# Two PSUM banks for q's projection, squares beside the norms, and a gate from the hyperbolic tangent

## What is computed

```
xn = layernorm(x)                              # x: 2 x 512 rows of 512
q, k, v = xn Wq^T, xn Wk^T, xn Wv^T            # 32 query heads, 8 key/value heads of 128
q, k = rmsnorm(q) * wq, rmsnorm(k) * wk        # t * (mean(t^2) + 1e-6)^-1/2 * w
attn = softmax(q k^T / sqrt(128) + causal ALiBi bias)
s    = (attn v) Wo^T
g    = silu(2 * sum_h (xn A_h^T) B_h^T * 8 softmax(xn Wr^T + br)_h)
y    = x + s * g
```

## Time and profile before

| | |
|---|---|
| time, median of 3 (lowest, highest) | 797.04 us (796.98, 799.42) |
| the profiled execution: its time, its span | 793.71 us, 791.6 us |
| mean granted clock of TensorE | 0.983 |
| busy: PE, PEld | 727.6 us (92%), 612.6 us (77%) |
| busy: DVE, ACT, POOL | 583.8 us (74%), 559.6 us (71%), 399.9 us (51%) |
| DMA | 148 MB, 187 GB/s, queue 64.7% of 16 engines |

### The profile page before, as it was taken

The page is one execution under the profiler, slowest core; times in us unless marked ns, Lnnn a source line. Parts: engine busy times, 40 slices in busy tenths (PEclk is TensorE's granted clock), DMA queues, the critical chain, the costliest instruction groups (busy, mean ns, idle before and its releaser), DMA issues.

```text
span 791.6 us, 14475 instructions
## 1 busy us (share of the span) xinstructions
PE 727.6 (92%) x3729; PEld 612.6 (77%) x3729; DVE 583.8 (74%) x1378; ACT 559.6 (71%) x1370; POOL 399.9 (51%) x423
## 2 busy tenths in 40 slices
PE   8888989999899999999899989999899998999697
PEld 7777867778788778887778778887787787787575
DVE  7855778677886778687877769778786778777555
ACT  4664767686676877777777876777686866768863
POOL 5313373555444762544644664445635554447347
PEclk9999999999999999999999999999999999999989
DMA  7014848678495767859485765858477784956642
GB/s 285 1 28 115 270 107 237 191 214 239 109 275 156 223 185 194 240 145 294 130 236 169 231 201 151 270 153 258 130 224 205 208 251 109 268 159 188 187 148 94
DMA packets 214772, 148.01 MB, mean 187 GB/s; under 512 B 48992, under 2 KB 205536, under 8 KB 214624
## 3 DMA queue, kind: packets, MB, share of 16 engines
q1 hardware_dynamic: 214752, 147.77, 64.7%
HBM read 85.84 MB, written 61.87 MB: 187 GB/s over the span
## 4 chain that ended last, share of the span: by engine, by line
PE 33%; issue 26%; POOL 24%; DVE 10%; ACT 4%; DMA 2%; POOLq 1%; SPq 1%; DVEq 0%; ACTq 0%
POOL pt_lo L529 10%; POOL inv_rms L519 8%; PE qkv_ps L1151 7%; PE qkv_ps L1152 6%; PE qkv_ps L1153 6%; POOL wo_lo L511 3%; DVE qk_norm L963 3%; DVE sums L947 2%; PE score_ps L1151 2%; PE score_ps L1153 2%; POOL sums_eps L517 2%; PE score_ps L1152 2%; PE out_ps L1151 2%; PE out_ps L1152 2%; PE out_ps L1153 2%
## 5 line engine op out<-in xcount | busy, mean ns | idle before, releaser
L529 POOL TENSOR_TENSOR pt_lo<-x_sb,pt_hi 128x512 fp32r<-128x512 f32 x153 | 195.3, 1303 | 240.8 <-ACT pt_hi L691 240.8
L1151 PE MATMUL qkv_ps<-w_hi,xt_hi 128*128 128x512 f32 (+1 forms) x512 | 182.0, 355 | 40.4 <-DVE qk_norm L963 38.4
L1152 PE MATMUL qkv_ps<-w_lo,xt_hi 128*128 128x512 f32 (+1 forms) x512 | 176.9, 345 | 0.0
L1153 PE MATMUL qkv_ps<-w_hi,xt_lo 128*128 128x512 f32 (+1 forms) x512 | 175.8, 343 | 0.0
L639 ACT ACTIVATE probs<-probs,neg_max 128x128 f32<-128x128 f32 (+3 forms) x256 | 141.7, 556 | 37.4 <-DVE neg_max L899 35.0
L1151 PEld LDWEIGHTS qkv_ps<-w_hi,xt_hi 128*128 128x128 f32 x512 | 99.2, 194 | 70.2 <-DVE qk_norm L963 34.6
L899 DVE CUSTOM_DVE_ANT_0 probs<-score_ps,cst,slope 128x128 f32<-128x128 f32 (+3 forms) x196 | 102.0, 545 | 54.1 <-PE score_ps L1153 46.1
L647 ACT ACTIVATE probs<-probs,recip 128x128 f32<-128x128 f32 (+3 forms) x252 | 122.2, 549 | 6.1 <-DVE recip L906 6.0
L918 DVE STREAM_TRANSPOSE squared<-probs 128x256 f32<-128x256 f32 (+3 forms) x124 | 99.7, 823 | 18.9 <-ACT probs L647 17.0
L1152 PEld LDWEIGHTS qkv_ps<-w_lo,xt_hi 128*128 128x128 f32 x512 | 99.6, 195 | 11.9
L1153 PEld LDWEIGHTS qkv_ps<-w_hi,xt_lo 128*128 128x128 f32 x512 | 99.2, 194 | 12.0
(11 more groups left out here) (166 smaller groups left out, 1444.7 us busy)
## 6 DMA issues: line engine op xcount, KB each, us to landing
turning_qk<-squares SPq DMA_DIRECT2D x240, 80.0 KB, 1.9
qk_moved<-turning_qk SPq DMA_DIRECT2D x60, 320.0 KB, 3.2
turning<-squared SPq DMA_DIRECT2D x120, 128.0 KB, 2.2
x_sb<-turning SPq DMA_DIRECT2D x30, 512.0 KB, 5.0
w_raw<-wqkv SPq DMA_DIRECT2D x32, 384.0 KB, 5.3
turning<-squared SPq DMA_DIRECT2D x120, 96.0 KB, 1.9
x_sb<-turning SPq DMA_DIRECT2D x30, 384.0 KB, 4.2
turning<-squared SPq DMA_DIRECT2D x128, 64.0 KB, 1.8
```

The costliest lines, as they stand in the source:

```text
L529: nc.gpsimd.tensor_tensor(by_quad(pt_lo, j), moved_block(t, j), by_quad(pt_hi, j).bitcast(F32), ALU.subtract).then_inc(pt_lo_by_pool, 1)
L1151: pe.matmul(out, a_hi, b_hi, start=start, stop=False)
L1152: pe.matmul(out, a_hi, b_lo, start=False, stop=False)
L1153: return pe.matmul(out, a_lo, b_hi, start=False, stop=stop)
```

## The change

Four things. First, from unit 6 on q's projection alternates between `turn_ps` (even units) and bank 0 of `qkv_ps` (odd units), with waits of its own: q's on the q norm two units back, k's and v's on the k norm of one unit back. All of q's chunks come before those of k and v, except for a group's block 0, where the chunks are taken two by two. Squares and norms are split in q and k. Second, the scores' head 3 leaves `turn_ps`: with one or two key blocks it takes half of `score_ps`'s bank 2, with more it shares bank 0 and waits. Third, `squares` has a column with 128 x eps behind each head, `qk_norm` lies in it, and `qk_squared` is a tile of its own. Fourth, gate = h (1 + tanh h) with h half the argument, by pairs of blocks: ACT's tangent in the last group's slots 3, 4, 5 and the end, DVE's product in slots 4 and 5 and twice in the end; POOL's `end` waits for all four.

In the prologue `normalize_qk(0, u)` becomes `normalize_k(0, u)` and `normalize_q(0, u)` at the same places; `qkv_ready` becomes `q_ready` and `kv_ready` (SP's waits take `kv_ready`), and `turn_q` and `turn_k` wait for q's and k's norm.

```diff
-squares = sb("squares", [NORMED * HD])
-qk_norm = sb("qk_norm", [NORMED, HD])
+
+squares = sb("squares", [NORMED, HD + 1])
+qk_norm = squares[:, :, 0:HD]
...
-qk_squared = squares[:, :].rearrange("p (k n) -> p k n", k=QUADS)
+qk_squared = sb("qk_squared", [QUADS, NORMED * QUAD])
...
-eps_sum = sb("eps_sum", [NORMED])
-sums_eps = sb("sums_eps", [NORMED])
...
+gate_tanh = wo_raw[:, 2:HPG, :]
...
-qkv_flat = qkv_ps[:, :, :].rearrange("p a n -> p (a n)")
-v_ps = qkv_flat[:, QK:QKV]
+k_ps = qkv_ps[:, 1, 0:HD]
+v_ps = qkv_ps[:, 1, HD:2 * HD]
...
+def q_ps(u):
+
+    return turn_ps[:, :] if two_banks(u) and u % 2 == 0 else qkv_ps[:, 0, :]
+
+def two_banks(u):
+    return u >= BY_TURN + 2
...
-def score_bank(t, h, at_end=False):
+def score_bank(t, h):
     n = keys_of(t) * P
-    if h == 3 and has_own_bank(t, at_end):
-        return turn_ps[:, 0:n]
+    if h == 3 and has_half(t):
+        return score_ps[:, 2, SEQ // 2:SEQ // 2 + n]
     return score_ps[:, h % (3 if t >= 2 else 2), 0:n]
-def has_own_bank(t, at_end=False):
-    return t > 2 and not at_end
+def has_half(t):
+    return t >= 2 and keys_of(t) <= 2
...
     nc.gpsimd.memset(minus_half[:, :], -0.5).then_inc(half_set, 1)
-    nc.gpsimd.memset(eps_sum[:, :], HD * RMS_EPS).then_inc(eps_set, 1)
+    nc.gpsimd.memset(squares[:, :, HD:HD + 1], HD * RMS_EPS).then_inc(eps_set, 1)
     nc.gpsimd.memset(acc[:, :, :], 0.0).then_inc(acc_ready, 1)
     pool.wait_ge(half_set, 1)
-    pool.wait_ge(eps_set, 1)
...
     def inverse_rms(g, u):
         pool.wait_ge(sums_ready, ONE(g, u, 1))
-        nc.gpsimd.tensor_tensor(sums_eps[:, :], sums[:, :], eps_sum[:, :], ALU.add).then_inc(eps_added, 1)
-        pool.wait_ge(eps_added, ONE(g, u, 1))
-        nc.gpsimd.tensor_tensor(inv_rms[:, :], sums_eps[:, :], minus_half[:, 0:NORMED],
+        nc.gpsimd.tensor_tensor(inv_rms[:, :], sums[:, :], minus_half[:, 0:NORMED],
                                 ALU.pow).then_inc(inv_rms_ready, 1)
         pool.wait_ge(inv_rms_ready, ONE(g, u, 1))
         pool.wait_ge(factor_set, g + (u // BLOCKS + 1))
...
     def end(g):
         turned_lo(g, BY_PE - 1)
-        pool.wait_ge(gate_done, 1)
+        pool.wait_ge(gate_done, BLOCKS // 2)
         pool.wait_ge(x_again, 16 * BLOCKS)
         for m in range(3):
...
         act.wait_ge(gate_in_done, t + 1)
-        nc.scalar.activation(gate[:, t, :], gate_ps[t][:, :], ACT.Copy, scale=FFN_SCALE).then_inc(gate_in_kept, 1)
-
-    def gates():
-
-        nc.scalar.activation(gate[:, :, :], gate[:, :, :], ACT.Silu).then_inc(gate_done, 1)
+        nc.scalar.activation(gate[:, t, :], gate_ps[t][:, :], ACT.Copy, scale=FFN_SCALE / 2).then_inc(gate_in_kept, 1)
+
+    def gate_tangents(k):
+
+        if k == 0:
+            act.wait_ge(wo_lo_done, GROUPS * HPG)
+        else:
+            act.wait_ge(gate_done, k)
+        nc.scalar.activation(gate_tanh, gate[:, 2 * k:2 * k + 2, :], ACT.Tanh).then_inc(gate_tanh_done, 1)
...
     def square_qk(g, u):
-        act.wait_ge(qkv_ready, ONE(g, u, 1))
-        if u > BY_TURN:
-            act.wait_ge(qk_written, QK_WRITTEN(g, u - BY_TURN, 0))
-        nc.scalar.activation(squares[:, :], qkv_flat[:, 0:QK],
+        act.wait_ge(q_ready, ONE(g, u, 1))
+
+        if 0 < u <= BY_TURN:
+            act.wait_ge(qk_turned, TWO(g, u, 0))
+        elif u > BY_TURN:
+            act.wait_ge(qk_squared_ready, ONE(g, u - BY_TURN, 0))
+        nc.scalar.activation(squares[:, 0:HPG, 0:HD], q_ps(u).rearrange("p (h d) -> p h d", h=HPG),
                              ACT.Square).then_inc(squares_ready, 1)
+        act.wait_ge(kv_ready, ONE(g, u, 1))
+        nc.scalar.activation(squares[:, HPG, 0:HD], k_ps, ACT.Square).then_inc(squares_ready, 1)
...
-        if left == 1 and t == SILU_SLOT:
-            gates()
+        if left == 1:
+            gate_tangents(t - 3)
...
         for n in range(keys_of(before)):
...
-        by_twos = t > 2 and not at_end and (h >= 2 or keys_of(t) <= 2)
+        by_twos = t > 2 and not at_end
         if not (by_twos and h % 2 == 1):
             dve.wait_ge(scores_ready, PER_HEAD(g, t, h + (2 if by_twos else 1)))
             if t > 0 and h % 2 == 0 and not at_end:
                 dve.wait_ge(probs_squared, TWO(g, t - 1, h // 2 + 1))
             dve.sem_inc(scores_taken, 1)
...
     def square_sums(g, u):
-        dve.wait_ge(squares_ready, ONE(g, u, 1))
-        nc.vector.tensor_reduce(sums[:, :], squares[:, :].rearrange("p (h d) -> p h d", h=NORMED), AX.X, ALU.add).then_inc(sums_ready, 1)
+        dve.wait_ge(squares_ready, TWO(g, u, 2))
+        if u == 0:
+            dve.wait_ge(eps_set, 1)
+        nc.vector.tensor_reduce(sums[:, :], squares[:, :, :], AX.X, ALU.add).then_inc(sums_ready, 1)
...
@@ -952,22 +970,25 @@
         dve.wait_ge(v_hi_ready, ONE(g, u, 1))
         nc.vector.tensor_tensor(v_lo[:, b, ui, :], v_ps, v_hi[:, b, ui, :].bitcast(F32), ALU.subtract).then_inc(v_lo_ready, 1)
-    def normalize_qk(g, u):
+    def normalize_k(g, u):
         dve.wait_ge(inv_ready, ONE(g, u, 1))
-
-        if u == BY_TURN:
-            dve.wait_ge(qk_turned, TWO(g, u, 0))
-        elif u > BY_TURN:
-            dve.wait_ge(qk_squared_ready, ONE(g, u - BY_TURN, 0))
-        nc.vector.tensor_tensor(qk_norm[:, :, :], qkv_flat[:, 0:QK].rearrange("p (h d) -> p h d", h=NORMED),
-                                inv[:, :].unsqueeze(2).broadcast_to([P, NORMED, HD]), ALU.mult).then_inc(qk_norm_ready, 1)
+        nc.vector.tensor_tensor(qk_norm[:, HPG, :], k_ps, inv[:, HPG:NORMED].broadcast_to([P, HD]),
+                                ALU.mult).then_inc(k_norm_ready, 1)
+
+    def normalize_q(g, u):
+
+        nc.vector.tensor_tensor(qk_norm[:, 0:HPG, :], q_ps(u).rearrange("p (h d) -> p h d", h=HPG),
+                                inv[:, 0:HPG].unsqueeze(2).broadcast_to([P, HPG, HD]), ALU.mult).then_inc(q_norm_ready, 1)
     def square_both(g, u):
-        dve.wait_ge(qk_norm_ready, ONE(g, u, 1))
-        nc.vector.transpose(qk_squared.rearrange("p k (h n) -> p h k n", h=NORMED),
-                            qk_norm[:, :, :].rearrange("p h (k n) -> p h k n", k=QUADS)).then_inc(qk_squared_ready, 1)
+        dve.wait_ge(q_norm_ready, ONE(g, u, 1))
+
+        if u > BY_TURN:
+            dve.wait_ge(qk_written, QK_WRITTEN(g, u - BY_TURN, 0))
+        nc.vector.transpose(qk_squared[:, :, :].rearrange("p k (h n) -> p h k n", h=NORMED),
+                            qk_norm.rearrange("p h (k n) -> p h k n", k=QUADS)).then_inc(qk_squared_ready, 1)
...
+
+    def multiply_gate(k):
+
+        dve.wait_ge(gate_tanh_done, k + 1)
+        nc.vector.scalar_tensor_tensor(out=gate[:, 2 * k:2 * k + 2, :], in0=gate_tanh, scalar=1.0,
+                                       in1=gate[:, 2 * k:2 * k + 2, :], op0=ALU.add, op1=ALU.mult).then_inc(gate_done, 1)
...
         if here(t + 2, left):
-            normalize_qk(g, t + 2)
+            normalize_k(g, t + 2)
         if (t + 3) % BLOCKS == 0 and here(t + 3, left):
             set_factor(g, t + 3)
         if here(t, left):
             reciprocals(g, t, 2)
         if here(t + 2, left):
+            normalize_q(g, t + 2)
             square_both(g, t + 2)
+        if left == 1 and t > 3:
+            multiply_gate(t - 4)
...
         add_out(g, before - 3)
+        multiply_gate(2)
         mixed_lo(g, before - 2, 1)
...
         reciprocals(g, last, 2)
+        multiply_gate(3)
         add_out(g, before - 1)
...
-    def project(g, t, chunks=range(KC)):
+    def project_q(g, t, c):
         m = t % BLOCKS
         rows = slice(m * P, (m + 1) * P)
-        if 0 in chunks:
-            if t > 0:
-                pe.wait_ge(qk_norm_ready, ONE(g, t - 1, 1))
-                pe.wait_ge(v_lo_ready, ONE(g, t - 1, 1))
+        if c == 0:
+            if two_banks(t):
+                pe.wait_ge(q_norm_ready, ONE(g, t - 2, 1))
+            elif t > 0:
+                pe.wait_ge(q_norm_ready, ONE(g, t - 1, 1))
             if t < 2:
                 pe.wait_ge(xt_lo_done, t + 1)
-        for c in chunks:
-            if t == 0:
-                pe.wait_ge(w_lo_done, c + 1)
-            elif m == 0 and c < EARLY_W:
-                pe.wait_ge(w_lo_by_dve, (g + t // BLOCKS - 1) * EARLY_W + (c + 1))
-            elif m == 0:
-                pe.wait_ge(w_lo_by_pool, (g + t // BLOCKS - 1) * (KC - EARLY_W) + (c - EARLY_W + 1))
-            for bank, lo, hi in ((0, 0, QW), (1, QW, QKV)):
-                last = three(qkv_ps[:, bank, 0:hi - lo], xt_hi[:, c, rows], xt_lo[:, c, rows],
-                             w_hi[:, c, lo:hi], w_lo[:, c, lo:hi], c == 0, c == KC - 1)
-            if m == BLOCKS - 1 and c < EARLY_W:
-                last.then_inc(w_left, 1)
-        if KC - 1 in chunks:
-            last.then_inc(qkv_ready, 1)
+        if t == 0:
+            pe.wait_ge(w_lo_done, c + 1)
+        elif m == 0 and c < EARLY_W:
+            pe.wait_ge(w_lo_by_dve, (g + t // BLOCKS - 1) * EARLY_W + (c + 1))
+        elif m == 0:
```

(47 more changed lines are left out.)

32 lines of the change are left out of this document (19 added, 13 removed).

## The result

The change makes the kernel slower: 829.55 us (median of 4; 826.52 to 831.13) against 797.01 (793.48 to 799.42) for the kernel before on the same chip, ratio 1.0373, 95% interval 1.0341 to 1.0406. 794.0 was predicted, with a range up to 803. The profiled execution has a span of 824.7 us (before 791.6).

What follows compares the result with a forecast made beforehand. The prediction took a loop chain through DMA, ScalarE, GpSimd and VectorE as the bound, not TensorE. Loop -9.4 and tail +6.4 (slot 5's -1.4 included) gave -3.0 us: 794.0 us, range 777 to 803.

Steps and rivals of the forecast that it cites:

- What bounds the kernel: Loop: a chain through DMA, ScalarE, GpSimd and VectorE sets the period; TensorE's 38.4 us stall is a side branch.
- Rival (A): Loop: TensorE is the bound after all, about 34 of its 38.4 us come off, 769 us; chance 0.13.
- The sum: Whole kernel: -9.4 in the loop and +6.4 in the tail make -3.0 us, so 794.0 us.
- What the split costs: Separate q and k instructions: VectorE +0.08 us per slot, in the chain; ScalarE +0.16 per slot, counted as 0.
- The added eps gone: Loop: GpSimd's add leaves the chain, 6.4 us in weight-split slots and 3.0 in other passages, together -9.4 us.
- Squares apart: Loop: ScalarE's squares no longer wait for DMA and come forward in slot 5; counted as 0.
- rival (C): The qk_moved round trip sets the loop, or head 3 eats the gain: loop 0, tail +6.4, 803.4 us; chance 0.19.
- Head 3 loses turn_ps: Scores: head 3 waits for head 0's bias, covered by other waits, 0; uncovered 22 us.
- The gate: Last group and tail: tanh gains 1.4 us in slot 5; GpSimd's gate work waits for the fourth product, net +6.4.
- (D): Tanh isn't in Exp's table, so each of four brings two loads of 1.28 us: 798 us; chance 0.06.

Runs made afterwards that it cites:

- the straight form: VectorE's seven loop turns written out instead of looped: 815.84 us on the changed kernel, 794.89 us on the kernel before.
- the shift: Changed kernel, loop unchanged, with 20 more semaphore increments on VectorE ahead of the loop: 818.07 us (1.0265).
- experiment 10: Changed kernel with VectorE's loop written out, q's norm directly behind k's, the factor's copy at slot 5's end and Silu in one piece: 799.98 us.
- experiment 8: Changed kernel, VectorE's loop written out, one bank of q: 826.29 us with q's norm late, 805.05 with it directly behind k's.
- experiment 7: VectorE's loop written out: kernel before with only the norms split, 813.05 us; changed kernel with q's norm directly behind k's, 806.49 us.
- experiment 5: Kernel before with only eps in the sum and squares apart: 800.70 us as a loop, 798.86 with VectorE's loop written out.

## Why the prediction was wrong

What the 32.5 us (829.55 - 797.01) are made of: the loop's place 13.7 (by the straight form; 11.5 by the shift), the order of the two norms 9.3, the gate 6.3 (7.3 on the kernel before), head 3's bank 3.1, the eps and the second bank 0: 32.4. Each term is a difference of medians. Those of the kernels with four runs are known to 5 or 6 us each (head 3's to 3), so a single term may be several us off; that the terms come to 32.4 is closer than that allows and partly luck. The straight form is also 3.7 us faster by itself on the kernel before, which has no pause, so the shift's 11.5 is the cleaner price of the loop's place. Best known is the sum of the first three, 29.6 us, since experiment 10 undid them together.

- **What bounds the kernel: right.** TensorE's 38.4 us were a side branch. They went, and nothing came of it (experiment 8). Rival (A), with 0.13, falls. But the branch lies close to the chain: with q's norm late, one bank instead of two cost 10.5 us.
- **The sum had no term for VectorE's code: the largest miss.** The prediction counted each instruction by its duration and none by its place. Nothing in the trace of before warned of it. A few instructions ahead of the loop's end decided over it: five more ahead of the loop and one more in it brought the pause, twenty more ahead took it away.
- **"What the split costs" failed.** The price of two instructions instead of one was right (0.29 and 0.67 us against 0.82, less their overlap). But the prediction priced the instructions and not the order: the reciprocals and the factor's copy had come between the two norms. That cost 9.3 us (experiment 7), not 0.08 a slot. The diff showed the order. The copy's 1.03 us in the trace of before (it wasn't among the rows) was itself the sign that it meets GpSimd's `w_lo`.
- **"The added eps gone" failed: -9.4 predicted, 0 measured.** It took the 0.99 us from `sums_eps` to `inv_rms` as a gain. The add went, but the chain from `pt_lo` to `inv` became only 0.13 us shorter in slot 5 (7.84 to 7.71). "Squares apart" failed with it: it saw the squares come forward in slot 5 and put that at 0, since GpSimd is in its subtractions. But it brings VectorE's weight split beside those subtractions, and they take 0.74 us longer for it (experiment 5). The 0.20 of the other slots met the `qk_moved` round trip, as the longer waits for it suggest and as rival (C) said.
- **"Head 3 loses turn_ps" at 0: too low by 3.1 us,** inside the bounds of 0 and 22.
- **The gate: mechanism right, size a little low.** One table load, products of 1.18 to 1.21 us, GpSimd's first gate product 1.29 us after the start of the fourth product, no pause behind it, the span's end 25.2 us on (25 predicted). +6.4 was forecast, with the -1.4 of slot 5 within it; +7.3 was measured. What was off is the gain in slot 5: TensorE's wait there fell from 6.81 only to 5.68 (`q_lo`, behind the first product, now met a `pt_lo` of GpSimd and took 1.40 us instead of 0.67), so the fourth product started at 772.67, not at 771.7, and the profiled span grew by 7.6 instead of 6.4. (D), other tables for the tangent, falls too.
- **Rival (C)** (the loop gives 0, the tail costs 6.4: 803.4) describes what gate, eps and banks do together. The sum of these parts alone, with head 3, would be 807. What lifted the time to 829.6 was in no rival.

The Trainium skill, "SBUF — State Buffer", says under "Reading the diagram" that VectorE and GpSimd share a port pair that one instruction holds for its whole length, while the other blocks fully. The trace agrees in form: `k_lo` 0.34 or 1.37 us by which of the two starts first, the copy of five numbers 0.15 or 1.57 (it ended about when the first of GpSimd's two `w_lo` did), and GpSimd's power 1.17 alone and 1.76 or 1.88 beside VectorE's `w_lo`.

## What to carry to other kernels

Before pricing an edit by its instructions, write down each engine's new order beside the old one and look at what now stands between two halves of a split step; a tiny instruction can be the long one if it meets the other engine's long one. A step that takes longer in one place than elsewhere may be held up by a neighbour; ask what runs beside it, and what an earlier start of the neighbour would run beside. And when a loop shows idle "issue" at its head, count the instruction queue's packets first; twenty added increments recovered 11.5 us here.
